# A recurrent memory of lines: blending a tile later, decay on ScalarE, sums of squares in another order

## What is computed

```python
write_lines = exterior(w1, w2); read_lines = exterior(r1, r2)   # 6 numbers per token and head, divided by their norm
Jw = einsum('bthi,ij->bhtj', write_lines, _J6); rd = transpose(read_lines, (0, 2, 1, 3))
outer = Jw[..., :, None] * Jw[..., None, :]                     # 6 x 6 per token and head
M_all = decayed sum of outer over all earlier tokens            # decays = sigmoid(decay_logits), one for each head
rd_M = einsum('bhti,bhtij->bhtj', rd, M_all)
score_M = sum(rd_M * rd, -1); score_M2 = sum(rd_M * rd_M, -1)
mem_score = (1 - alpha) * score_M + alpha * score_M2            # alpha = sigmoid(iter_mix)
gated = mean(sigmoid(mem_score * mem_scale) * gate, -1)
out = (seq_out + gated * mem_val) @ out_w.T + out_b
```

## Time and profile before

| | us |
|---|---|
| median of 3 runs | 1938.73 |
| lowest and highest of them | 1938.09, 1938.75 |
| profiled execution, its own time | 1937.65 |
| its span in the trace | 1935.8 |
| PE busy in the span | 1876.7 |
| DVE busy | 1609.8 |
| ACT busy | 1500.5 |
| POOL busy | 918.2 |

### The profile page before, as it was taken

The page is one execution under the profiler, slowest core; times in us unless marked ns, Lnnn a source line. Parts: engine busy times, 40 slices in busy tenths (PEclk is TensorE's granted clock), DMA queues, the critical chain, the costliest instruction groups (busy, mean ns, idle before and its releaser), DMA issues. The chain is left out here.

```text
span 1935.8 us, 61266 instructions
## 1 busy us (share of the span) xinstructions
PE 1876.7 (97%) x22612; PEld 1114.6 (58%) x22612; DVE 1609.8 (83%) x5464; ACT 1500.5 (78%) x4122; POOL 918.2 (47%) x550
## 2 busy tenths in 40 slices
PE   7999999999999989999999999899999999999999
PEld 3777763577775343444444358536777635777754
DVE  6899975899995679999999859869999658999945
ACT  5999994799997353777777754459999947999973
POOL 2788860588882040000000036428888505888820
PEclk9999999999999996999999999999999999999999
DMA  6212220122121040111111000002122201221311
GB/s 186 49 44 50 46 67 6 31 48 50 45 65 26 6 154 29 42 41 42 42 42 41 25 6 2 2 10 53 45 49 49 64 6 32 47 50 44 68 23 44
DMA packets 76154, 85.63 MB, mean 44 GB/s; under 512 B 17151, under 2 KB 50515, under 8 KB 75731
## 3 DMA queue, kind: packets, MB, share of 16 engines
q1 hardware_dynamic: 75663, 81.70, 16.8%
q10 hardware_dynamic: 196, 0.02, 0.0%
HBM read 21.16 MB, written 8.39 MB: 15 GB/s over the span
## 5 line engine op out<-in xcount | busy, mean ns | idle before, releaser
L336 ACT ACTIVATE probs<-probs,negmax 128x128 f32<-128x128 f32 x1024 | 402.0, 402 | 1.1 <-DVE negmax L411 0.6
L2289 ACT ACTIVATE gprobs<-ps_global 128x1024 f32<-128x1024 f32 (+3 forms) x384 | 291.4, 811 | 125.0 <-PE ps_global L1754 102.4
L291 POOL TENSOR_TENSOR rot<-rot 128x1024 f32<-128x1024 f32 x128 | 302.5, 2363 | 143.2 <-DVE rot L381 143.2
L297 POOL TENSOR_TENSOR qk<-rot,cnorm 128x1024 f32<-128x1024 f32 x128 | 243.8, 1905 | 172.8 <-issue 149.0
L304 POOL TENSOR_TENSOR probs<-probs,iden 128x1024 f32<-128x1024 f32 x128 | 242.8, 1897 | 45.7 <-DVE iden L419 45.0
L1984 DVE TENSOR_REDUCE maxes<-ps_global 128x1 f32<-128x512 f32 (+2 forms) x384 | 222.0, 638 | 10.3 <-PE ps_global L1717 6.5
L411 DVE CUSTOM_DVE_ANT_0 probs<-ps_attn,masks 128x128 f32<-128x128 f32 x1024 | 226.2, 285 | 0.7 <-issue 0.5
L336 ACT ACTIVATION_READ_ACCUMULATOR probs<-probs,negmax 128x1 f32 x1024 | 204.7, 200 | 0.0
L1712 PE MATMUL ps_global<-kq 48*128 48x512 bf16 (+3 forms) x768 | 196.9, 345 | 7.2 <-DVE maxes L1984 1.8
L2219 POOL CAST m_parts<-m_turn 32x128 bf16<-32x128 f32 x16 | 4.5, 280 | 363.3 <-DVE m_turn L1998 363.3
L377 DVE TENSOR_TENSOR rot<-ps_attn,rotary 128x512 f32<-128x512 f32 x256 | 174.9, 683 | 2.1 <-PE ps_attn L202 1.6
(11 more groups left out here) (228 smaller groups left out, 4529.9 us busy)
## 6 DMA issues: line engine op xcount, KB each, us to landing
v_first<-v_second SPq DMA_DIRECT2D x256, 128.0 KB, 2.3
hs<-z_a SPq DMA_DIRECT2D x256, 32.0 KB, 1.9
ln<-z_b SPq DMA_DIRECT2D x56, 128.0 KB, 2.5
kq<-split_scratch SPq DMA_DIRECT2D x64, 96.0 KB
kq<-split_scratch SPq DMA_DIRECT2D x64, 64.0 KB
split_scratch<-parts SPq DMA_DIRECT2D x8, 384.0 KB, 4.1
split_scratch<-gprobs SPq DMA_DIRECT2D x6, 384.0 KB, 4.1
x_tok<-in_x_dram SPq DMA_DIRECT2D x4, 512.0 KB, 6.4
```

Source lines behind the costliest of these rows:

```text
L291: nc.gpsimd.tensor_tensor(a, a, b, ALU.add).then_inc(C["rot_sum"], 1)
L297: nc.gpsimd.tensor_tensor(qk[:, k % 2, :].rearrange("p (h d) -> p h d", d=DH), rot_a[:, k % 2, :, :], cnorm[:, k % 2, :].unsqueeze(2).to_b ...
L336: last = nc.scalar.activation(probs[:, k % 2, slot, :], probs[:, k % 2, slot, :], ACT.Exp, scale=-1.0, bias=negmax[:, k % 2, slot:slot + 1 ...
L2289: nc.scalar.activation(probs[:, step % RING, 2 * p:2 * p + 2, 0:w], ps[:, S0 + 2 * p:S0 + 2 * p + 2, 0:w], ACT.Exp).then_inc(C["p2_exp"], 1)
```

## The change

Six edits, all in this pass:

- DVE: `weigh(t-1)` now stands in body t between the last `terms` and `sum_squares(t + 2, 0)`; before, `weigh(t)` stood behind the last two multiplies of body t. For the last tile, `weigh(7)` follows behind the second half of its sum, as before. `read` gets two buffers for it.
- DVE: the second half of `read_memory` follows the last two multiplies, where it stood ahead of them.
- DVE: `advance` stands ahead of `clip(t + 2, 0)` and `sum_squares(t + 2, 1)`. From tile 1 on it is two additions of 288 elements, the decayed state (`faded`) plus the tails.
- ACT: a new `fade(t + 1)` makes the decayed state, four instructions of 144 elements, behind `copy_scores` in body t.
- DVE: `clip(., 1)` of tile t+2 moves out of body t into body t+1, behind the first multiply and the first `terms`.
- ACT: `scale_lines(t)` moves from behind the fifth copy to behind the eighth.

```diff
@@ class storage
+        faded = squares[:, :, :].rearrange("p k t -> p (k t)")[:, 0:GROUPS * STATE_ROWS].rearrange("p (q n) -> p q n", q=GROUPS)
-        read, plain, blend = [behind.take(HB * LINE).rearrange("p (x c) -> p x c", x=HB) for _ in range(3)]
+        read = behind.take(2 * HB * LINE).rearrange("p (k x c) -> p k x c", k=2, x=HB)
+        plain, blend = [behind.take(HB * LINE).rearrange("p (x c) -> p x c", x=HB) for _ in range(2)]
@@ DVE advance(k)
+                if k > 0:
+                    wait(dve, "ml_faded", k)
+                    for half in range(2):
+                        at = slice(half * GROUPS // 2, (half + 1) * GROUPS // 2)
+                        last = nc.vector.tensor_tensor(state[:, (k + 1) % 2, at, :].rearrange("p q n -> p (q n)"),
+                                                       faded[:, at, :].rearrange("p q n -> p (q n)"),
+                                                       ps[:, TAIL_BANKS[half], 0:2 * STATE_ROWS], ALU.add)
+                    last.then_inc(C["ml_state"], 1)
+                    return
@@ DVE body(t)
                 multiplies(0, 1)
                 all_terms(0, 1)
+                if 1 < t + 1 < S_TILES:
+                    clip(t + 1, 1)
                 multiplies(1, 2)
...
                 all_terms(5, 6)
+                if valid(t - 1):
+                    weigh(t - 1)
                 if valid(t + 2):
                     sum_squares(t + 2, 0)
+                multiplies(6, 8)
                 if valid(t):
                     read_memory(t, 1)
-                multiplies(6, 8)
-                if valid(t):
+                if t == LAST:
                     weigh(t)
+                if t + 1 < LAST:
+                    advance(t + 1)
                 if valid(t + 2):
                     clip(t + 2, 0)
                     sum_squares(t + 2, 1)
-                if t + 1 < LAST:
-                    advance(t + 1)
-                if valid(t + 2):
-                    clip(t + 2, 1)
@@ ACT
+            def fade(k):
+                wait(act, "ml_state", k)
+                for q in range(GROUPS):
+                    last = nc.scalar.activation(faded[:, q, :], state[:, k % 2, q, :], ACT.Identity, scale=A["whole"][:, q:q + 1])
+                last.then_inc(C["ml_faded"], 1)
@@ ACT body(t)
                 if valid(t - 2):
                     copy_scores(t - 2)
-                lefts(2, 5)
-                if valid(t):
-                    scale_lines(t)
-                lefts(5, 6)
+                if 0 < t + 1 < LAST:
+                    fade(t + 1)
+                lefts(2, 6)
                 if valid(t + 2):
                     square_line(t + 2, 0)
                 lefts(6, 8)
+                if valid(t):
+                    scale_lines(t)
```

More of the change, by code:

```diff
@@ L1560, in global_attention_pass @@
             "ml_outer", "ml_tail", "ml_state", "ml_row0", "ml_row1", "ml_m", "ml_term", "ml_read", "ml_plain", "ml_blend", "ml_weight",
-            "ml_score", "ml_turned", "ml_out"))
+            "ml_score", "ml_turned", "ml_out", "ml_faded"))
     U2 = P2_STEPS
@@ L2031, in read_memory @@
                 wait(dve, "ml_term", USES_M * k + (3 if half == 0 else USES_M))
-                nc.vector.reduce_sum(read[:, first * B:end * B, :].rearrange("p x c -> p (x c)"),
+                nc.vector.reduce_sum(read[:, k % 2, first * B:end * B, :].rearrange("p x c -> p (x c)"),
                                      term[:, first * B * PAIRS_6:end * B * PAIRS_6].rearrange("p (x j) -> p x j", j=LINE), AX_X
@@ L2038, in weigh @@
                 wait(dve, "ml_plain", k + 1)
-                flat = read[:, :, :].rearrange("p x c -> p (x c)")
+                flat = read[:, k % 2, :, :].rearrange("p x c -> p (x c)")
                 nc.vector.scalar_tensor_tensor(out=blend[:, :, :].rearrange("p x c -> p (x c)"), in0=flat, scalar=A["alpha"][:, 0:1],
```

## The result

The changed kernel takes 1942.25 us, median of 19 runs (1940.14 to 1946.08), the kernel before 1937.77 us, median of 19 runs. The ratio is 1.0027, which is 5.2 us, with a 95% interval of 1.0021 to 1.0034, 4.1 to 6.6 us. The forecast was 1943.4 us and 4.7 us slower, in a range of 1940.0 to 1946.5.

The account below looks back on a forecast made before the run. The prediction took a loop through POOL, PE, ACT and DVE as the bound, not DVE alone. Six turns at +0.2 us and the tail at +4.5 on 1938.73 gave 1943.4 us, range 1940.0 to 1946.5.

Parts of the forecast that it names:

- Half a turn from last multiply to clip 1: In each turn, start of the last multiply to the second clip: 4.54 us, 0.23 later than before.
- The wait ahead of the first multiply: DVE idle 1.1 us ahead of a body's first multiply, for ACT's copy queued behind Ln and Exp.
- The other half: Clip 1 to last multiply: 8.22 us by PE and ACT, 8.40 by DVE; 8.51 before.
- The additions: State's step on DVE: two additions, each moving the next start by 0.36 us, 0.72 together, instead of 1.10.
- The decay: ACT's four instructions, 1.1 to 1.4 us, from about 4.2; third copy (0.36) behind, wanted about 5.9; costed at nothing.
- Reciprocal and clip 1 of tile 7: Behind the turns: clip 1 follows the reciprocal, at 6.42 instead of 4.31 us; outer products at 7.50 instead of 5.39.
- Memory of tile 7: PE behind the turns: waits for the outer products' row by DMA, at 15.12 us instead of 13.01.
- The lock holds the blend of tile 5 ... ahead of the memory's DMA: hidden: Behind the turns: blend held some 1.3 us behind POOL's outer products of tile 7, at no cost.
- turn(6) and mean(1): PE behind the turns: waits for score 6 until 23.5 us instead of 19.05; mean(1) at 29.3, 4.5 later.
- The faster case: Rival: DVE is the bound, six turns give -7 us, tail +4.5: 1936 or 1933 us; chance 0.10.
- The case of a half-covered tail: Rival: slack in PE's queue behind turn(6) leaves only 2.1 or 2.8 us: 1941.0 to 1941.7; chance 0.22.
- The case of ACT's instructions being too long: Rival: at 0.6 us each they delay the third copy, +0.3 to +0.5 a turn, 1945.5 to 1946.5; chance 0.11.

Follow-up runs that it names:

- the runs on clip 7 and score 5: Each the changed kernel with one edit: tile 7's second clip ahead of the reciprocal, 1.0022; tile 5's score ahead of body 6's first half of sums, 1.0026.
- the fastest one: Changed kernel with its tail moves undone and ACT's first two copies of the next body ahead of Ln and Exp; 1932.48 us, 0.9964 of the kernel before.

## Why the prediction was right, and where it was not

**The turn.** Right in mechanism, and near in every term. Half a turn from last multiply to clip 1: 4.54 forecast, 4.54 measured. The wait ahead of the first multiply: 1.1 and 1.00. The other half between its bounds of 8.22 and 8.40: 12.84 - 4.54 = 8.30. The additions: 0.81 for the two together, as two `terms` of 288 would be. The decay: 1.33 us for four, within its 1.1 to 1.4, and covered, but only just: the third copy ends at 1178.86 and the third multiply starts at 1178.96. The prediction let this cover go from some 0.4 us an instruction; by its own terms (4.2, 0.36 and 5.9) it goes from 0.34.

**Reciprocal and clip 1 of tile 7.** Right: clip 1 at 6.42 forecast and 6.39 measured, outer products at 7.50 and 7.48.

**Memory of tile 7.** 15.12 forecast, 15.68 measured. The step that failed is "The lock holds the blend of tile 5 ... ahead of the memory's DMA: hidden". The blend was held for 1.0 us; what I left out is that turn(5) and the spread stand between that score and memory 7 on PE. turn(5) came at 13.16 instead of 10.94, and PE, at half clock behind a wait of 3.3 us, took 1.02 and 1.91 us for them instead of 0.60 and 1.02. The two chains end within 0.6 us of each other (the outer products at 7.48 and the prediction's 7.62 for their row put its own wait at 15.10), so the total hardly showed it; the runs on clip 7 and score 5, where my expectations failed, did.

**turn(6) and mean(1).** The mechanism was right, the size 0.8 too small: turn(6) 23.5 forecast, 24.37 measured, 5.76 us to `mean(1)` in both. 0.56 of this comes from memory 7.

**What was left out.** PE's clock. The gate projection behind the tail at half clock is 1.6 us in the profiled execution of the changed kernel, and the output projections at the end of the pass, at half clock in the trace of the kernel before alone, give 0.95 back. The prediction handed the delay at `mean(1)` on in full and had neither. `mean(1)` was 5.3 us later and not 4.5, so that the medians came out within 0.3 us of the forecast 4.7 is partly luck; by the ratio the difference is 5.2, by the two profiled executions 6.5.

**The rivals.** The faster case failed on its condition: the first multiply does wait. The case of a half-covered tail failed, since there is no slack behind turn(6): 5.76 us back to back. The case of ACT's instructions being too long failed by their 0.33 us each, close to the 0.34 from which they would have cost something.

## What to carry to other kernels

An engine that is 95% busy in a stage needn't be its bound if a loop runs through it and three others: what counts is the work that stands between the wait and the release on that loop. Here 0.38 us less in each turn in one place and two copies moved in another were worth 1.9 and 4.9 us of the first half. The 1.6 us that the whole change took from DVE in each turn came back in the same turn as waits of 1.00 and 0.6. A move by one tile is cheap in the steady turns and has to be followed into the bodies at the end by itself, for each queue: who there waits for the late result, and what is queued behind that one. Where two engines lock each other out, ask which instruction of the other one runs at the new place, not only at the old.

## What was new about the hardware

The record of a blocked instruction holds its wait: a blend of 0.61 us was recorded as 0.80, 1.22, 1.62 and 4.39 us, each time ending 0.41 or 0.42 us behind the end of POOL's instruction. The excess over 0.61 on such a row is a wait, which the column of idle time doesn't show.

The granted clock of PE followed its waits within this stage. In the changed kernel and in the fastest one (columns as in the earlier trace rows: window, PE, PEld, DVE, ACT, POOL, granted clock):

```profile
1234.30:1237.50 3.20, 0.00 (x0) 0.00 (x0) 3.13 (x6) 1.09 (x2) 1.60 (x1) 0.97 0.00 1
1237.50:1240.30 2.80, 2.75 (x7) 1.43 (x8) 1.10 (x1) 1.74 (x4) 1.26 (x1) 0.50 0.01 2
...
1257.80:1261.40 3.60, 3.52 (x4) 0.97 (x5) 0.03 (x1) 0.68 (x1) 0.83 (x1) 0.53 0.00 0
```

```profile
1227.20:1230.00 2.80, 2.25 (x13) 1.40 (x13) 2.77 (x5) 1.68 (x4) 1.26 (x1) 1.00 0.01 2
...
1230.00:1250.00 20.00, 17.41 (x63) 7.47 (x62) 16.05 (x25) 8.10 (x13) 3.77 (x3) 1.00 0.00 0
```

Behind the 3.2 us in which PE did nothing the changed kernel's matmuls run at 0.50, which is 1.2 GHz, and the spread takes 1.91 us instead of 1.02; the fastest kernel stays at 1.00, 2.4 GHz, through the same stretch, which begins with its turn(5) at 1227.20. A wait of PE thus cost more than its length here, about 1.3 us more in the two steps behind the one for score 5. It doesn't always: behind the 1.18 us wait ahead of the gate projection the changed kernel is at 0.53 and the kernel before, behind the same wait, at 1.00 (1251.80 to 1255.40).
